# A buffer each for the first six patch tiles, and their steps moved by one

## The reference

```python
z = layernorm(patches, ln1) @ W_proj + b_proj        # 64 x 36 patches of 768 numbers -> 256
z = layernorm(z, ln2_g, ln2_b)
h = concat([cls, z]) + pos_emb ; h = concat([h, txt])  # 64 sequences of 69 tokens of 256
xn = layernorm(h); q, k, v = xn @ wq.T, xn @ wk.T, xn @ wv.T   # 16 heads of 16, rotary on q, k
h = h + softmax(q k^T / 4) v
xn2 = layernorm(h); top 2 of 8 experts by xn2 @ router, softmax over the two
h = h + sum of weight * (silu(xn2 @ gate) * (xn2 @ up)) @ w2   # hidden 512
```

## Time and profile before

| what | value |
|---|---|
| median of 3 runs | 854.26 us (851.39 to 857.37) |
| profiled execution | 846.84 us, its span 845.1 us |
| first 50 us (prologue: patch tiles 0 to 5, first sequence tiles) | PE busy 32.74, DVE 37.46, POOL 34.78, ACT 11.52 us |
| 50 to 380 us (attention, one sequence after another) | PE busy 300.57, DVE 267.72, ACT 236.26, POOL 179.27 us |
| rest (routing, then 76 expert tiles) | untouched by the change |

### The profile page before, as it was taken

How to read it: one execution, slowest core, us unless ns; L and a number is a source line. 1 busy time by engine, 2 the same in 40 slices (tenths; PEclk the granted TensorE clock), 3 DMA queues, 4 the chain that set the end, 5 groups by cost and what they waited for, 6 DMA issues and landing times. The chain is left out here.

```text
span 845.1 us, 27607 instructions
## 1 busy us (share of the span) xinstructions
PE 722.3 (85%) x9892; PEld 507.0 (60%) x9892; DVE 562.1 (67%) x1164; ACT 397.5 (47%) x881; POOL 443.6 (52%) x613
## 2 busy tenths in 40 slices
PE   5768989998999999889502499999999999999993
PEld 4636666766777777667301266666666666656662
DVE  6978988886888888775389455555555555555552
ACT  1234676776788777777200133333333333333331
POOL 6742555665566664633317345555556555555652
PEclk9968999999999999998555599999999999999998
DMA  8676574545655555444100033333333333333332
GB/s 297 203 242 222 183 237 130 156 142 164 185 161 151 154 163 146 123 139 117 42 7 1 20 50 58 60 56 56 60 65 55 61 59 57 60 56 65 56 60 26
DMA packets 64872, 91.80 MB, mean 109 GB/s; under 512 B 13176, under 2 KB 45704, under 8 KB 64679
## 3 DMA queue, kind: packets, MB, share of 16 engines
q1 hardware_dynamic: 49655, 66.81, 25.8%
q0 software_dynamic: 15088, 23.21, 15.7%
HBM read 58.95 MB, written 24.10 MB: 98 GB/s over the span
## 5 line engine op out<-in xcount | busy, mean ns | idle before, releaser
L1252 POOL DMA_INDIRECT out<-y,token_of x76 | 120.6, 1586 | 137.6 <-DMA out<-y,token_of 127.4
L1297 DVE SCALAR_TENSOR_TENSOR hid<-quad,up_scale,silu 128x512 f32<-128x512 f32 x76 | 57.1, 751 | 99.6 <-PE quad L1333 97.1
L1333 PE MATMUL quad<-w_hi,x_hi 128*128 x304 | 116.0, 381 | 1.1 <-DVE x_lo L1304 1.1
L1333 PE MATMUL quad<-w_lo,x_hi 128*128 x304 | 115.8, 381 | 0.0
L1333 PE MATMUL quad<-w_hi,x_lo 128*128 x304 | 115.7, 381 | 0.0
L526 DVE TENSOR_REDUCE nm_src<-quad 69x16 f32<-69x1104 f32 x64 | 83.0, 1297 | 34.9 <-PE quad L822 34.8
L710 ACT ACTIVATE probs<-quad 69x1104 f32<-69x1104 f32 x64 | 69.7, 1088 | 52.8 <-PE quad L905 52.8
L1265 ACT ACTIVATE hid_hi<-bank 128x512 f16<-128x512 f32 x76 | 45.4, 597 | 104.2 <-PE bank L1352 104.2
L1245 POOL DMA_INDIRECT xg<-xn_rows,token_of x76 | 75.6, 995 | 35.1 <-issue 18.0
L1277 ACT ACTIVATE x_hi<-bank 128x256 f16<-128x256 f32 x76 | 29.2, 384 | 119.6 <-PE bank L1373 119.6
L1333 PE MATMUL bank<-w_hi,hid_hi 128*128 x304 | 82.9, 273 | 1.6 <-ACT hid_hi L1265 1.6
(11 more groups left out here) (213 smaller groups left out, 1858.5 us busy)
## 6 DMA issues: line engine op xcount, KB each, us to landing
w_lo<-in_experts_w SPq DMA_DIRECT2D x24, 512.0 KB, 6.1
w_raw<-in_experts_w SPq DMA_DIRECT2D x48, 256.0 KB, 4.6
xt<-in_patches SPq DMA_DIRECT2D x18, 384.0 KB, 5.8
h<-h_rows SPq DMA_DIRECT2D x34, 128.0 KB, 5.5
hb<-h_rows SPq DMA_DIRECT2D x34, 128.0 KB, 5.8
out<-h SPq DMA_DIRECT2D x34, 128.0 KB, 4.3
xn_rows<-xn SPq DMA_DIRECT2D x34, 128.0 KB, 4.8
vb<-v SPq DMA_DIRECT2D x30, 138.0 KB
```

Source lines behind the costliest of these rows:

```text
L1252: nc.gpsimd.indirect_dma_start(out, bass.IndirectOffsetOnAxis(token_of[:, n:n + 1], 0), y[q][:, :], None, compute_op=ALU.add).then_inc(add ...
L1297: nc.vector.scalar_tensor_tensor(out=hid[q][:, :], in0=quad[:, 2 * q + 1, :], scalar=up_scale[:, :], in1=silu[q][:, :], op0=ALU.mult, op1= ...
L1333: last = nc.tensor.matmul(dst, x[:, k, :], w[:, bass.ds(col + k * (2 * width if width == HIDDEN else width), width)], start=(k == 0 and m ...
```

## The change

The six early patch tiles get a buffer each for their finished rows: `zout0`, `zout1`, and, since these are not in use yet, `xn20`, `xn21`, `h20`, `h21`. Their steps move one later (`EARLY`), with START (-12 becomes -11) and what hangs on it; the parts keep their steps, counted in t. The store of the first six moves from step m+3 to m+2, so that its step number stays what it was, and behind the `shift` load. POOL finishes tile n (L435, L438 before) ahead of the small operations for tile n+1 instead of behind them, and behind those for `rs3` of the same step. ACT normalises tile n ahead of the evacuation of `xT` in that step. ACT's wait for the store of tile n-2 is gone for the first six; SP waits for it instead before it stores tile n. The first users of `xn2` and `h2` wait for those stores.

```diff
--- before.py
+++ after.py
@@ -39,8 +39,8 @@
 TXT_STEP = [None, 1, 9]
 LAST_STEP = BATCH + 8
 CHUNK_FROM = 17
-PART_FROM = 3
-EARLY = [-10, -9, -8, -7, -6, -5]
+PART_FROM = 2
+EARLY = [-9, -8, -7, -6, -5, -4]
 EARLIEST = len(EARLY)
 
 
@@ -138,6 +138,11 @@
                 denom = tb("denom", [P, HEADS])
                 xn2T = tb("xn2T", [P, KD, P])
                 w_raw = ring("w_raw", [P, W_CHUNK], n=3)
+                early_rows = [*zout, *xn2, *h2]
+                assert len(early_rows) == EARLIEST
+
+                def patch_rows(n):
+                    return early_rows[n] if n < EARLIEST else zout[n % 2]
 
                 names = """ones_set pow_set consts_in bias_in gain_in qkv_in rope_in router_in pos_in pos_added cls_in cls_added
                     sel_col parity_set sel_set tables_set zeroed pads_set spare_zero wg_ready wide_ready bias_mm col_mm bias_ready wc_ready
@@ -271,6 +276,13 @@
                                     sp.wait_ge(s["xn_ready"], g - 1)
                                 sp.dma_start(h[g % 2][0:rows[g], :], h_rows[P * g:P * g + rows[g], :]).then_inc(h_in[g % 2], 16)
 
+                        def store_patches(n):
+                            sp.wait_ge(s["zout_ready"], n + 1)
+                            if 2 <= n < EARLIEST:
+                                sp.wait_ge(z_stored[n % 2], 16 * z_count[n - 2])
+                            for at, row, k in segments(n):
+                                sp.dma_start(h_rows[row:row + k, :], patch_rows(n)[at:at + k, :]).then_inc(z_stored[n % 2], 16)
+
                         def step(t):
                             for n in chunk_step.get(t + 1, ()):
                                 if n >= 3:
@@ -286,14 +298,12 @@
                                 if g >= 2:
                                     sp.wait_ge(s["h2_ready"], g - 1)
                                 sp.dma_start(hb[g % 2][0:rows[g], :], h_rows[P * g:P * g + rows[g], :]).then_inc(hb_in[g % 2], 16)
-                            behind = t in HL and t - 3 in ZM and last_patch_tile[HL[t]] >= ZM[t - 3]
+                            later = t - 3 in ZM and ZM[t - 3] >= EARLIEST
+                            behind = t in HL and later and last_patch_tile[HL[t]] >= ZM[t - 3]
                             if not behind:
                                 load_h(t)
-                            if t - 3 in ZM:
-                                n = ZM[t - 3]
-                                sp.wait_ge(s["zout_ready"], n + 1)
-                                for at, row, k in segments(n):
-                                    sp.dma_start(h_rows[row:row + k, :], zout[n % 2][at:at + k, :]).then_inc(z_stored[n % 2], 16)
+                            if later:
+                                store_patches(ZM[t - 3])
                             if behind:
                                 load_h(t)
                             if t - 1 in ZM:
@@ -304,6 +314,8 @@
                                     sp.wait_ge(s["zout_ready"], n - 1)
                                 at = P * n % PATCHES
                                 sp.dma_start(shift[n % 2][:, :], pos_rows[at:at + P, :]).then_inc(shift_in[n % 2], 16)
+                            if t - 2 in ZM and ZM[t - 2] < EARLIEST:
+                                store_patches(ZM[t - 2])
                             b = t + 1
                             if 0 <= b < BATCH:
                                 g = tile_of(SEQ * b + SEQ - 1)
@@ -378,6 +390,15 @@
                             pool.wait_ge(rstd_ready, n + 1)
                             nc.gpsimd.tensor_scalar(off, mv, rs, -1.0, ALU.mult, ALU.mult).then_inc(signal, 1)
 
+                        def finish_patches(n):
+                            if n == 0:
+                                pool.wait_ge(s["gain_in"], 16)
+                            pool.wait_ge(s["zn_ready"], n + 1)
+                            nc.gpsimd.tensor_tensor(patch_rows(n)[:, :], patch_rows(n)[:, :], gain[:, :], ALU.mult).then_inc(s["zg_ready"], 1)
+                            pool.wait_ge(s["zg_ready"], n + 1)
+                            pool.wait_ge(shift_in[n % 2], 16 * (n // 2 + 1))
+                            nc.gpsimd.tensor_tensor(patch_rows(n)[:, :], patch_rows(n)[:, :], shift[n % 2][:, :], ALU.add).then_inc(s["zout_ready"], 1)
+
                         pool.wait_ge(s["pow_set"], 1)
 
                         def step(t):
@@ -389,6 +410,8 @@
                                 if g >= 2:
                                     pool.wait_ge(s["xn2_ready"], g - 1)
                                     pool.wait_ge(out_stored[g % 2], 16 * (g // 2))
+                                else:
+                                    pool.wait_ge(z_stored[g], 16 * z_count[4 + g])
                                 nc.gpsimd.tensor_tensor(h2[g % 2][0:r, :], hb[g % 2][0:r, :], att[0:r, :], ALU.add).then_inc(s["h2_ready"], 1)
                             if t in PJ:
                                 g = PJ[t]
@@ -419,6 +442,8 @@
                                     pool.wait_ge(s["xn2_ready"], g - 1)
                                 rstd(ve4[0:r, :], mv4[g % 2][0:r, 1:2], rs4[g % 2][0:r, :], g, s["eps4"], s["rstd4"])
                                 offset(off4[g % 2][0:r, :], mv4[g % 2][0:r, 0:1], rs4[g % 2][0:r, :], g, s["rstd4"], s["off4_ready"])
+                            if t - 2 in ZM and ZM[t - 2] < EARLIEST:
+                                finish_patches(ZM[t - 2])
                             if t - 1 in ZM:
                                 n = ZM[t - 1]
                                 pool.wait_ge(s["mv2_ready"], n + 1)
@@ -427,15 +452,8 @@
                                     pool.wait_ge(s["zn_ready"], n)
                                 rstd(ve2[:, :], mv2[:, 1:2], rs2[:, :], n, s["eps2"], s["rstd2"])
                                 offset(off2[:, :], mv2[:, 0:1], rs2[:, :], n, s["rstd2"], s["off2_ready"])
-                            if t - 2 in ZM:
-                                n = ZM[t - 2]
-                                if n == 0:
-                                    pool.wait_ge(s["gain_in"], 16)
-                                pool.wait_ge(s["zn_ready"], n + 1)
-                                nc.gpsimd.tensor_tensor(zout[n % 2][:, :], zout[n % 2][:, :], gain[:, :], ALU.mult).then_inc(s["zg_ready"], 1)
-                                pool.wait_ge(s["zg_ready"], n + 1)
-                                pool.wait_ge(shift_in[n % 2], 16 * (n // 2 + 1))
-                                nc.gpsimd.tensor_tensor(zout[n % 2][:, :], zout[n % 2][:, :], shift[n % 2][:, :], ALU.add).then_inc(s["zout_ready"], 1)
+                            if t - 2 in ZM and ZM[t - 2] >= EARLIEST:
+                                finish_patches(ZM[t - 2])
                             if t + 1 in ZM:
                                 n = ZM[t + 1]
                                 pool.wait_ge(s["mv1_ready"], n + 1)
@@ -655,6 +673,13 @@
                         def chunks(ap, n):
                             return ap.rearrange("p (c n) -> p c n", c=n)
 
+                        def norm_patches(n):
+                            act.wait_ge(s["off2_ready"], n + 1)
+                            if n >= EARLIEST:
+                                act.wait_ge(z_stored[n % 2], 16 * z_count[n - 2])
+                            nc.scalar.activation(patch_rows(n)[:, :], z[n % 2][:, :], ACT.Identity,
+                                                 bias=off2[:, :], scale=rs2[:, :]).then_inc(s["zn_ready"], 1)
+
                         def step(t):
                             if t in XT:
                                 g = XT[t]
@@ -700,6 +725,8 @@
                                 if g >= 2:
                                     act.wait_ge(s["xn2_turned"], g - 1)
                                     act.wait_ge(xn_stored[g % 2], 16 * (g // 2))
+                                else:
+                                    act.wait_ge(z_stored[g], 16 * z_count[2 + g])
                                 nc.scalar.activation(xn2[g % 2][0:r, :], h2[g % 2][0:r, :], ACT.Identity,
                                                      bias=off4[g % 2][0:r, :], scale=rs4[g % 2][0:r, :]).then_inc(s["xn2_ready"], 1)
                             b = t - 2
@@ -742,6 +769,8 @@
                                 if g == 0:
                                     act.wait_ge(s["pads_set"], V_RING + 3)
                                 evac(logits[0:r, g, :], b5[0:r, KD * P:KD * P + EXPERTS], s["logits_saved"])
+                            if t - 2 in ZM and ZM[t - 2] < EARLIEST:
+                                norm_patches(ZM[t - 2])
                             if t + 1 in ZM and ZM[t + 1] < EARLIEST:
                                 n = ZM[t + 1]
                                 act.wait_ge(s["xT0_turned"], n + 1)
@@ -759,13 +788,8 @@
                                 n = ZM[t + 1]
                                 act.wait_ge(s["xT1_turned"], n + 1)
```

(9 more changed lines are left out.)

## The result

| | changed kernel | kernel before, same chip |
|---|---|---|
| median of 20 runs | 857.62 us | 855.03 us |
| lowest to highest | 853.10 to 867.73 us | 844.17 to 863.40 us |
| profiled execution (span) | 857.04 us (855.2) | 846.84 us (845.1) |

The ratio of the times is 1.0054, 95% interval 1.0030 to 1.0077. It is taken from the fast runs alone, without the few in the slower state that this program falls into at times. On 855 us it is 4.6 us slower, 2.6 to 6.6: a real loss, and within 1%. The forecast was 857.3 us, 850.5 to 862. The medians differ by 2.6 us, but the two profiled executions by 10.1 us of span, more than twice what the ratio says. So the profile gives the places, and the ratio gives the size.

What follows compares the result with a forecast made beforehand. It took POOL's queue, then DVE's, as the bound in the prologue; the early gain becomes idle time, and DVE's 3.0 us delay gives 846.84 + 3.0 = 849.8 us profiled, 857.3 on the runs' scale, range 850.5 to 862.

Steps and rivals of the forecast that it cites:

- Carried to the end: From DVE's wait for sequence tile 3's h onward, its queue is full, so the 3.0 us stay to the end.
- POOL's order and the removed waits: Prologue: ACT's 7.4 us of waits count as nothing; POOL's new order gains 2.1 us, 1.0 left at the rotary sum.
- signs of being wrong: No DVE wait for tile 3's h, POOL not busy unbroken from 37 to 49 us, or DVE's tile 5 statistics earlier.
- The first projection: PE's first projection, waiting for sequence tile 1's xn, starts at 44.3 instead of 46.37 us.
- The late piece: POOL's long operations for patch tile 5 end at 54.6, delaying their store and tile 3's h load; DVE 3.0 us later.
- The landing term: The load of h for sequence tile 3, issued at 57.7, lands 4.8 us later, at 62.5.
- late is late for good: From 57 to 67 us DVE is busy 9.62 of 10 us, so any lateness there is never recovered.
- second wait: Not in the forecast sum: DVE's wait for h of sequence tile 4, 6.98 us in the changed kernel.
- slower by more: Rival: parts and h of sequence tiles 3 and 4, issued later, land in 9.0 us; +7.2 us, 861.5; chance 0.13.
- PE's clock: Addition to the slower rival: PE falls to 1.2 GHz during DVE's wait, up to 5 us more, 866.5; chance 0.05.
- A gain: Rival: sequence tile 3's h is not late enough to matter; 1.0 to 2.1 us stay, 852.2 to 853.3; chance 0.2.

Runs made afterwards that it cites:

- e4: Kernel before with a buffer each for the six early patch tiles and their waits on SP, no instruction moved: ratio 0.9999.
- e1: Changed kernel with SP's store of patch tile 5 moved behind the load of h for sequence tile 3 and the first vb load: ratio 0.9981.
- e2: Changed kernel with POOL's two long operations for patch tile 5 ahead of the three small ones for sequence tile 2: ratio 1.0042.
- f1: Changed kernel with weight parts 9 to 12 loading only an eighth of their width: ratio 0.9988.
- f4: Changed kernel with the edits of e1 and f2 together: ratio 0.9965, median 849.01 against 852.05 us.
- e3: Kernel before with only POOL's two long operations for patch tile 5 put behind the rotary sum and sequence tile 2's small operations: ratio 1.0078.
- e8: Kernel before with the second text load (768 KB) issued at step 3 instead of step 1: ratio 0.9983.
- f3: Kernel before with SP issuing the loads of h for sequence tiles 4 and 5 a step sooner: ratio 0.9990.
- f2: Changed kernel with SP issuing the loads of h for sequence tiles 4 and 5 a step sooner: ratio 1.0055.

## Why the prediction held, and where it was thin

**Luck in the number.** The forecast was worked out on the scale of the profile, 846.84 + 3.0 = 849.8 us, and the profiled execution took 857.04. On the scale of the runs 857.3 met a median of 857.62. The mechanism below held; that the number fits to 0.3 us is luck, since the steps of the trace add up to more than twice the difference of the runs, for reasons given under "Carried to the end".

**POOL's order and the removed waits: right.** ACT's waits at nothing (e4: 0.9999); in the changed kernel ACT waits for POOL's offsets instead, 14.6 us in six waits before its normalisations of patch tiles, where it waited 2.2 for them before. DVE's statistics of sequence tile 0 were forecast for 36.1 and came at 37.22; the whole prologue ran a microsecond later than I reckoned, which I had no term for. Every later point is shifted by about that: POOL's triple at 44.2 for 43.0, the first projection at 45.19 for 44.3, the rotary sum at 50.49 for 49.5. I had 1.0 us left there, and nothing was. The late microsecond is in the trace, far ahead of the change, in six DVE operations that neither kernel alters. In the kernel before, in its third profiled execution, and in the changed kernel:

```profile
9.43 1.74 DVE L475 TENSOR_SCALAR w_lo<-ones,b 128x128 f32<-128x128 f32 x6
```

```profile
9.57 4.03 DVE L475 TENSOR_SCALAR w_lo<-ones,b 128x128 f32<-128x128 f32 x6
```

```profile
9.88 3.57 DVE L493 TENSOR_SCALAR w_lo<-ones,b 128x128 f32<-128x128 f32 x6
```

The two lengths change from execution to execution of one kernel, so the lost microsecond says nothing against the new order. One of my signs of being wrong was there in part all the same: from about 37 to 49 us POOL waited twice, 0.99 us for DVE and 0.72 for ACT, and from 33 to 49.4 us it was busy 12.50 us instead of 14.39.

**The first projection: an unexpected help of no use.** PE had less idle time ahead of it (1.75 us before its last turn, where it was 3.48), and ran it at 2.4 GHz:

```profile
45.19 0.38 PE L811 MATMUL bank<-wqkv_hi,fx_hi 128*128 128x512 f16 x1
```

0.38 us where it was 0.63 at 46.37. In e1, e2, f1 and f4, which begin as the changed kernel does, the granted clock from 45 to 50 us was 0.50 to 0.53 against 0.95 here, so this front end does not always bring the faster level. The second half waited for `fx_lo` until 48.75 all the same, behind a DVE instruction that waited 2.25 us for POOL. A faster PE in front of a DVE queue that waits for POOL gives nothing.

**The late piece: right, by mechanism and by size.** Pair 5 at 55.2 for 54.6, the load at 58.49 for 57.7, DVE at 62.66 for 62.5, 3.2 us behind the kernel before for 3.0. e3 shows that it is sufficient and e1 that without it the loss is gone. The landing term, 4.8 us, was 4.1.

**Carried to the end: right, but the yardstick was a fast one.** I took "late is late for good" from DVE's 9.62 of 10 busy microseconds. The trace agrees, and further than sequence 8. The lag at sequences 8 and 48 is 10.5 and 11.2 us in the changed kernel, 9.9 and 9.4 in e3, 4.8 and 3.8 in e4, 3.7 and 3.9 in f1, 5.6 and 4.8 in f3: over these forty sequences the attention stage takes at most 1 us back. Behind sequence 48 most runs gain 2.6 to 4.2 us on the yardstick, but another execution of the kernel before does so too (from -0.1 at sequence 48 to -4.3 at the last), so that is a slow stretch of the yardstick itself.

What remains is that e4, e8, f1, f3 and f4 show a lag of 3.7 to 5.6 us at sequence 8 and ratios of 0.9965 to 0.9999, while the change, e2, e3 and f2 show 7.2 to 10.5 us and 1.0042 to 1.0078. That is what would be seen if a usual run of the kernel before were itself some 5 us behind its profiled executions; only e1, with a lag of -0.2 us and a ratio of 0.9981 and not less, does not fit. These took 846.2, 846.8 and 850.6 us, all below the medians of the runs beside them (854.4 and 855.0), and two things that could make up such a difference are on record: the six DVE operations above, short in two of the three, and the second wait, which none of the three has and e8 has. It is not shown for the unprofiled runs, since the place of a wait is only seen in a profiled execution.

**The second wait: missing from the sum.** It is the rival "slower by more", at its own place: the landings of the loads issued some 4 us later. I priced it as one long landing for tile 3's h (9.0 us). In truth tile 3's load landed in 4.1 us, and that of tile 4, at the end of the crowd, in 14.4. The rival's point, "where the landing exceeds about 5 us", was put on the wrong load. I had given this 0.13; the profile after has its wait in full, and the ratio, 4.6 us, lies between my 3.0 and its 7.2, nearer to 3.0. What the step "part 9 to 11 and h of sequence tiles 3 and 4 are all issued some 4 us later" lacked is that they are also issued closer together.

**PE's clock: a result, not a cause.** It stands at 0.50 from 68 to 86 us, behind a DVE wait of 7 us in which PE had nothing to do, in the changed kernel; in e3, with the same waits, it is 0.53, and in e1, with a wait of 2.5 us, 0.89. The lag grows by 1.7 us between sequences 3 and 8, and that is all that the rows leave for the clock; I had allowed 5. (Earlier, from 50 to 55 us, the clock may well be a cause: see e8.)

**A gain: fell, but it was there to be had.** e1 and f4 have it, 1.6 and 3.0 us in the mean; the first is not clear of nothing. The rival needed the store out of the way, and the change did not do that.

## What to carry to other kernels

When an operation moves back in one engine's order, follow it through the queue that hands its result on: there a store that nobody needs soon can hold up a load that the bound engine needs next, and the cure is the place of the store in that queue, not a faster producer. A queue that is released late, or that finds its waits already over, issues what has piled up in one burst, and a transfer near the end of it can land much later than the delay itself; advancing one of them here only changed which one was awaited. Removing waits on an engine that is not the bound (7.4 us here) brought nothing that could be measured. One profiled execution of each kernel can be off by twice the true difference: look at a second one of the kernel before, before its points in time are used as a yardstick.

## What the runs showed of the hardware

The same load of 128 KB out of the same buffer took 3.2 us, 4.8, 4.1 and 14.4 us to land, all in the prologue. With an eighth of the bytes in the four parts around it the slowest took 7.4. The granted clock from 68 to 86 us was 0.50 and 0.55 in the two profiles of the changed kernel, 0.53 in e3 and 0.51 in f2, where DVE waited 5.8 to 7.3 us within that stretch; 0.67 in e4, whose wait of 6.6 us ended at 72.24; and 0.88 in the kernel before and 0.89 in e1, where waits of 0.9 and 2.5 us had ended by 67.8.

A small POOL instruction took 2.12 us where it usually takes 0.57, beside one long DVE instruction with two inputs. POOL and DVE in the changed kernel:

```profile
30.78 2.12 POOL L387 TENSOR_TENSOR rs<-ve,eps_pow 128x1 f32<-128x1 f32 x1
```

```profile
30.65 1.82 DVE L524 SCALAR_TENSOR_TENSOR wqkv_lo<-w_lo,scale,wqkv_hi 128x1536 f16<-128x1536 f32 x1
```

It began 0.13 us behind the DVE instruction, which ended at 32.47, and was done 0.43 us after that. In the kernel before the same DVE instruction meets a long addition on POOL, from 28.58, which also takes 2.12 us for 0.72: the move changed which POOL instruction is caught, not that one is. The Trainium skill (SBUF — State Buffer, SBUF: two separate sides) says that a DVE instruction with two SBUF inputs and a GpSimd instruction that reads SBUF lock each other out of a shared pair of ports, and that the one that starts later is fully blocked. The trace agrees here: the POOL instruction ends 0.43 us after the other's end, somewhat less than its own usual 0.57. In the kernel before it agrees only in part: there a POOL multiplication begun 0.06 us behind the DVE instruction took its usual 0.73 us, and the DVE instruction took 2.40 us instead of 1.82, so by the recorded starts the earlier one was held up.
